# Three narrow attentions: products with values in pieces between transposition tiles, evacuated behind them

## What is computed

```python
attn = jnp.einsum('bkhd,bnhd->bhkn', q, kmat) / DH
attn = jnp.where(full_mask[:, None, None, :], attn, -jnp.inf)
attn = jax.nn.softmax(attn.astype(jnp.float32), axis=-1)
attn_out = jnp.einsum('bhkn,bnhd->bkhd', attn, v).reshape(b, k_len, H)
attn_out = attn_out @ out_w + out_b + residual
...
vh = jnp.concatenate([vh, jnp.broadcast_to(bias_v, (b, 1, H, K))], axis=1)   # layer 1
ctx = jnp.einsum('bhqt,bthk->bqhk', weights, vh).reshape(b, q_len, H * K)
return ctx @ wo + bo
```

## Time and profile before

| | us |
|---|---|
| median of three runs | 1074.5 |
| lowest and highest | 1072.48 and 1076.6 |
| the profiled execution | 1073.68 |
| its span, first to last instruction | 1071.9 |
| mean granted TensorE clock | 0.947 |

### The profile page before, as it was taken

How to read it: one execution, slowest core, us unless ns; L and a number is a source line. 1 busy time by engine, 2 the same in 40 slices (tenths; PEclk the granted TensorE clock), 3 DMA queues, 4 the chain that set the end, 5 groups by cost and what they waited for, 6 DMA issues and landing times. The chain is left out here.

```text
span 1071.9 us, 17946 instructions
## 1 busy us (share of the span) xinstructions
PE 946.0 (88%) x6616; PEld 802.6 (75%) x6616; DVE 774.2 (72%) x1625; ACT 604.4 (56%) x1371; POOL 312.3 (29%) x321
## 2 busy tenths in 40 slices
PE   4889886899999999999799999998487899779958
PEld 4766665788999999998689999997476666656647
DVE  3486766468878888886688888877674788558864
ACT  3587883236555655554455656555334787268842
POOL 3454550050221122221121122200004455445510
PEclk8899998999999999999899999999798799889989
DMA  4996005140110011111010011000306820394020
GB/s 147 273 232 97 2 1 197 60 159 1 40 40 5 36 41 40 41 40 41 1 40 6 35 40 40 1 1 1 124 1 158 208 46 2 106 242 64 1 85 20
DMA packets 39490, 72.71 MB, mean 68 GB/s; under 512 B 6534, under 2 KB 23944, under 8 KB 37228
## 3 DMA queue, kind: packets, MB, share of 16 engines
q1 hardware_dynamic: 39404, 71.56, 25.0%
HBM read 55.28 MB, written 16.27 MB: 67 GB/s over the span
## 5 line engine op out<-in xcount | busy, mean ns | idle before, releaser
L1316 ACT CAST L1a_probsT_hi<-L1a_bank 128x512 fp32r<-128x512 f32 x128 | 68.9, 589 | 84.6 <-PE L1a_bank L1194 84.5
L1152 POOL TENSOR_SCALAR L1a_wo_hi<-L1a_stage 128x512 fp32r<-128x512 f32 x16 | 10.4, 652 | 344.4 <-PE L1a_sums L74 336.5
L1351 ACT ACTIVATE L1a_probs<-L1a_scores,L1a_neg_max 128x512 f32<-128x512 f32 x128 | 86.8, 684 | 26.7 <-DVE L1a_bias_shifted L1441 22.1
L1437 DVE TENSOR_REDUCE L1a_top<-L1a_scores 128x2 f32<-128x1024 f32 x64 | 78.1, 1221 | 18.6 <-PE L1a_scores L74 18.6
L1374 DVE TENSOR_TENSOR L1a_probsT_lo<-L1a_bank,L1a_probsT_hi 128x512 fp32r<-128x512 f32 x128 | 82.0, 681 | 0.2
L1318 ACT ACTIVATE L1a_attended_hi<-L1a_bank,L1a_cols 128x256 fp32r<-128x256 f32 x64 | 30.5, 477 | 90.6 <-PE L1a_bank L74 90.6
L72 PE MATMUL L1a_bank<-L1a_probsT_hi,L1a_v_hi 128*128 128x256 f32 x256 | 73.1, 285 | 9.1 <-DVE L1a_probsT_lo L1374 9.1
L72 PE MATMUL L1a_bank<-L1a_w_hi,ctxT_hi 128*128 128x256 f32 x256 | 74.8, 292 | 0.3 <-DVE L1a_k_lo L1376 0.3
L417 POOL TENSOR_SCALAR L0a_probs<-L0a_probs,L0a_inverse 128x768 f32<-128x768 f32 x64 | 57.2, 906 | 57.8 <-DVE L0a_inverse L686 57.8
L74 PE MATMUL L1a_bank<-L1a_probsT_hi,L1a_v_lo 128*128 128x256 f32 x256 | 72.4, 283 | 0.0
L73 PE MATMUL L1a_bank<-L1a_probsT_lo,L1a_v_hi 128*128 128x256 f32 x256 | 72.4, 283 | 0.0
(11 more groups left out here) (410 smaller groups left out, 3083.4 us busy)
## 6 DMA issues: line engine op xcount, KB each, us to landing
L1a_stage<-in_L_w SPq DMA_DIRECT2D x15, 1024.0 KB, 4.8
L0m_fold_wq<-in_L_wqT SPq DMA_DIRECT2D x2, 2048.0 KB, 12.9
L0a_k_dram<-L0a_kT_hi SPq DMA_DIRECT2D x8, 384.0 KB, 10.2
L0a_k_stack<-L0a_k_dram SPq DMA_DIRECT2D x4, 576.0 KB
L0a_w_qkv<-L0a_k_dram SPq DMA_DIRECT2D x4, 576.0 KB
L0a_wide_wo<-in_L_wo SPq DMA_DIRECT2D x1, 2048.0 KB, 17.2
L0a_wide_wo<-in_L_wo SPq DMA_DIRECT2D x2, 1024.0 KB, 17.7
L0m_stage<-in_L_wm SPq DMA_DIRECT2D x4, 512.0 KB, 6.4
```

Of the source, the lines that this page charges most:

```text
L1316: nc.scalar.copy(out, source).then_inc(ring.hi_done, 1)
L1351: nc.scalar.activation(probs[:, g % 2, qt, :], scores[:, qt, :], ACT.Exp, bias=neg_max[:, g % 2, qt:qt + 1], accum_out=row_sum[:, g % 2, q ...
L1437: link(nc.vector.tensor_reduce(top[:, :], scores[:, :, :], AX.X, ALU.max))
```

## The change

A product is now split into `tj` pieces. For t = 5, 9, .. 29 (now `product_beside(t)`), PE writes transposition tile 0 of head t, piece 0 of the product, tile 1, piece 1, and so on. The product keeps one bank, but its job number comes behind the tiles of head t. On ACT and DVE its evacuation stands behind that of the tiles of head t. The values of the bias are split into one job for each of the two attentions of layer 1 (`bias_beside`, t = 14 and 15), in pieces as well, each with a copy of its own. `probsT` gets a sixth slot, since head t is written while the product still reads the unit.

```diff
-        TSLOTS = 5
+        TSLOTS = 6
...
-        def product_before(t):
+        def product_beside(t):
 
             return t // 4 - 1 if t % 4 == 1 and t >= 4 else None
 
 
-        BIAS_UNIT = 2
+        def bias_beside(t):
+
+            return t - 14 if cfg["bias_values"] and t in (14, 15) else None
+
         order = []
         for t in range(HEADS):
-            if product_before(t) is not None:
-                order.append(("V", product_before(t), 0))
-                if cfg["bias_values"] and product_before(t) == BIAS_UNIT:
-                    order.append(("B", 0, 0))
             order += [("T", t, c) for c in range(tj)]
+            if product_beside(t) is not None:
+                order.append(("V", product_beside(t), 0))
+            if bias_beside(t) is not None:
+                order.append(("B", bias_beside(t), 0))
         order.append(("V", units - 1, 0))
...
+            def values_of_bias(i, piece, pieces):
+                job = job_of["B", i, 0]
+                if piece == 0:
+                    pe.wait_ge(spread_ready, 1)
+                    pe.wait_ge(wide_loaded, 16 * 3)
+                    ring.wait_bank(pe, job)
+                for c in range(piece * 4 // pieces, (piece + 1) * 4 // pieces):
+                    for j in range(4):
...
                     last.then_inc(ring.full, 1)
+                    if unit is not None:
+                        product_v(unit, c, tj)
+                    if bias_layer is not None:
+                        values_of_bias(bias_layer, c, tj)
+
+            def product_v(unit, piece=0, pieces=1):
                 job = job_of["V", unit, 0]
-                ring.wait_bank(pe, job)
                 b, quad = divmod(unit, quads)
-                for back in range(ring.n):
-                    ring.wait_evacuated(pe, unit_copies(unit)[-1 - back])
-                for kt in range(nkt):
+                if piece == 0:
+                    ring.wait_bank(pe, job)
+                    for back in range(ring.n):
+                        ring.wait_evacuated(pe, unit_copies(unit)[-1 - back])
+                for kt in range(piece * nkt // pieces, (piece + 1) * nkt // pieces):
...
             def evacuate(t):
 
-                if product_before(t) is not None:
-                    high_v(product_before(t))
...
                 for c in range(tj):
                     if by_act(t, c):
                         job = job_of["T", t, c]
...
+                if product_beside(t) is not None:
+                    high_v(product_beside(t))
+                if bias_beside(t) is not None:
+                    job = job_of["B", bias_beside(t), 0]
+                    act.wait_ge(ring.full, job + 1)
+                    nc.scalar.copy(keep["bias_values"][:, bias_beside(t), :], ring.bank(job)[:, 0:D]).then_inc(ring.freed_by(job), 1)
...
                 if t >= 0:
-                    if product_before(t) is not None:
-                        low_v(product_before(t))
                     for c in range(tj):
                         if not by_act(t, c):
...
+                    if product_beside(t) is not None:
+                        low_v(product_beside(t))
```

More of the change, by code:

```diff
@@ L452, in _, with transpose_head @@
                 last.then_inc(ring.full, 1)
[L454 to L457, removed]
-                ring.wait_bank(pe, job)
[L459 to L467, removed]
+            def values_of_bias(i, piece, pieces):
[6 more added lines that the diff above has]
+                    for j in range(4):
+                        h = 4 * j + c
+                        last = nc.tensor.matmul(ring.bank(job)[32 * j:32 * j + 32, 0:D], spread[:, i, h, :],
+                                                wide_wo(i * H + h), start=c == 0, stop=c == 3)
+                if piece == pieces - 1:
+                    last.then_inc(ring.full, 1)
+            def transpose_head(g, unit, bias_layer):
                 pe.wait_ge(normed, 2 * g + 2)
@@ L476, in transpose_head @@
                     last.then_inc(ring.full, 1)
-            def product_v(unit):
+                    if unit is not None:
[3 more added lines that the diff above has]
+            def product_v(unit, piece=0, pieces=1):
                 job = job_of["V", unit, 0]
-                ring.wait_bank(pe, job)
                 b, quad = divmod(unit, quads)
-                for back in range(ring.n):
-                    ring.wait_evacuated(pe, unit_copies(unit)[-1 - back])
-                for kt in range(nkt):
+                if piece == 0:
[3 more added lines that the diff above has]
+                for kt in range(piece * nkt // pieces, (piece + 1) * nkt // pieces):
                     for j in range(4):
@@ L490, in product_v @@
                                                 moving, start=kt == 0, stop=kt == nkt - 1)
-                last.then_inc(ring.full, 1)
+                if piece == pieces - 1:
+                    last.then_inc(ring.full, 1)
             for g in range(HEADS + LAG):
@@ L508, in _ @@
                 if t >= 0:
-                    if product_before(t) is not None:
[L510 to L513, removed]
+                    transpose_head(t, product_beside(t), bias_beside(t))
             product_v(units - 1)
```

## The result

The changed kernel takes 1094.9 us (median of 4 runs, 1091.6 to 1098.4), the kernel before 1073.5 beside it (4 runs, 1067.4 to 1076.6): a ratio of 1.020, 95% interval 1.017 to 1.023. It is slower by 21.4 us. The forecast was 1099, its range 1083 to 1107.

The account below looks back on a forecast made before the run. It took PE to be near its limit in L0a, and ACT and DVE to bound L2a and L3a. Terms of 9.2 + 7.8 + 7.8 = 24.8 us on 1073.7 gave 1098.5, forecast as 1099, range 1083 to 1107.

Parts of the forecast that it names:

- first periods of L2a and L3a: First period of L2a and L3a, bank free: changes of form plus `low_v` make 0.8 us (0.5 to 1.1) each.
- Waiting for POOL, L0a: L0a: tile 0 now stands first and waits for POOL's multiplication, which the product used to cover; 0.36 us a period.
- Changes of form, L0a: L0a: three pairs of changes between transposition and product instead of one; two more at 0.27, 0.54 us a period.
- `low_v` ahead of the maxima, L0a: L0a: evacuation right before the next maxima starts them 1.10 us behind their scores, 0.45 us later each period.
- The seventh product and the end of L0a: L0a, t = 29: product ends later and DVE passes `low_v` before the last reciprocal; 1.5 us more.
- Bias values: L0a: bias values split over two heads lengthen the period by 3.05 us instead of 3.43, a gain of 0.4.
- The bank, L2a and L3a: L2a, L3a: piece 0 waits for a bank that ACT frees two exponentials later; maxima 1.06 us later, five periods 5.3.
- The ends of L2a and L3a: L2a, L3a, seventh product: late bank delays head 30's transposition, last product and output follow in series; 1.7 us each.
- The bank not late: Rival: ACT runs closer to PE, so L2a and L3a pay nothing and L0a pays 9.2; 1083 us, chance 0.11.
- Hidden: Rival: the waits fall into slack, above all in L0a, and earlier copies pay the rest; 1074 us, chance 0.05.
- faster: Rival: DVE's idle 1.21 us before `low_v` goes in 12 periods of L2a and L3a; 1060 us, chance 0.03.
- The clock falls: Rival: PE's clock drops at the new 1.2 to 1.4 us wait, 1.0 in 12 periods; 1111 us, chance 0.05.

## Why the prediction was right, and where it was off

The direction, the range and the main mechanisms were right. The sum was 24.8 us, and 21.4 were measured. A part of this closeness is luck: L0a came out 1.2 us above its sum, L2a and L3a together 3.1 below theirs. The step that is furthest off is the smallest in the argument: the first periods of L2a and L3a.

- **Waiting for POOL, L0a.** Predicted 0.36. Measured: from scores to tile 0 115.59 - 113.80 = 1.79, and before from scores to product 124.73 - 123.33 = 1.40; 0.39. Right.
- **Changes of form, L0a.** Predicted two pairs at 0.27, 0.54 in all. The two pairs cost 0.56 to 0.58 (pieces ahead of the tiles, whole products behind them), and three more pairs 0.86. But after has one entry more that shows: before, the one entry stood ahead of the product, in time in which tile 0 now waits for POOL anyway, so all three entries of after are visible. 4.76 - 4.01 = 0.75 is three entries and two exits. I had counted pairs, where I should have counted what stands behind the wait: 0.2 a period too little. The gaps that I expected in PE's rows are not there; they are in those of the weight loads.
- **`low_v` ahead of the maxima, L0a.** Predicted 0.45 (maxima 1.10 behind the scores). Measured: 1.05 behind them and 0.40 from scores to scores, and 0.38 come back when `low_v` is moved. Right, a little too high. The three together: 0.39 + 0.75 + 0.40 = 1.54, and 1.50 is the period's growth; predicted 1.35.
- **The seventh product and the end of L0a.** Predicted 1.5. From the last exponential to `w_out` 12.11 instead of 10.42: 1.7.
- **Bias values.** Their price fell from 3.43 to 3.16; predicted 3.05. Right in kind. The other form, whole and behind the tiles, shows what pieces took of it: 2.06 above its own period.
- **The bank, L2a and L3a.** Predicted +1.06 a period; measured +0.91, in both. The step that failed is the hand-over. I took the product's start, 0.21 behind ACT's copy, for the time from a copy to PE, and put it behind the new copy as well. But there PE was still at the scores issued at 865.88; the copy had been done. The rival of the bank that is not late was weighed with the same reading. A real hand-over is 0.05 (880.47 to 880.52). 1.06 - 0.16 = 0.90. The repaired bank gives 1.00 back.
- **The ends of L2a and L3a.** Predicted 1.7; from the last exponential to `w_out` 8.55 instead of 7.00: 1.55. The same 0.16 is in it.
- **The first periods of L2a and L3a.** Predicted +0.8 each. With five periods at 0.91 and the end taken out, 7.27 - 4.55 - 1.55 = 1.2 is left in L2a, and 5.23 - 6.10 = -0.9 in L3a. The waits of PE show what differs there, stretch of L2a to L3a, after:

```profile
PE L2a_scores L515 <- DMA L2a_q_stack<-L2a_q_dram: 7.2, 2, 3.9
PE L2a_bank L497 <- ACT L2a_probsT L585: 6.2, 6, 1.0
...
PE L3a_scores L515 <- DMA L3a_q_stack<-L3a_q_dram: 5.3, 2, 3.2
```

Before, the waits for these transfers were 5.1 and 6.8 us. The change moves no transfer. L2a's wait is 2.1 longer and L3a's 1.5 shorter, and in the experiments too these two stretches begin with waits of different length. So a part of L3a's 2.6 us and of the 1.4 elsewhere is this execution's share of luck with the transfers, not the change's. I can't say how it divides.

**The rivals.** *The bank not late* fell: PE waits 6.2 us for it in each of the two stretches, and repairing it gives 10 us back. *Hidden* and *faster* fell with it. What *faster* counted on, the idle 1.21 us of DVE before `low_v`, is still there (0.85). *The clock falls* did not happen in the profiled execution of the changed kernel, in these stretches behind the first product, but see the last section. The estimate that the prediction made from the Trainium skill's 175 ns (TensorE: Matmul & The Clock Gate, "Single matmul latency"), 0.35 for a pair and 1102 in all, is too high: six pieces gave 0.29 for each pair.

## What to carry to other kernels

In a ring of buffers the place in the order of jobs is also a choice of buffer: when a job moves behind two others, look up whose release it now needs, and when the engine that releases it comes to it. If that is late, the job can be given another place in the ring without moving any work, which gave 10 us here. Put long work of old data where the engine would wait for new data, not behind that wait, and don't let an evacuation stand directly in front of the operation that starts the next chain. Cutting work into pieces of another array form costs a fixed price for each change, which was hidden here only where the array had time to spare.

## What the runs showed of the hardware

- A change between full 128-column transposition tiles and 32-column quarter tiles costs about 0.15 us going in and 0.13 to 0.135 coming out, for pieces of 4 and of 8 matmuls alike (a matmul here is two of the records counted behind x). With all 24 matmuls in one, before, it was 0.12 coming out, and 0.16 going in from scores. PE's records show no idle time there; the price is in the steps between starts. The weight loads' records idle 0.17 us going in and 0.41 coming out. What the price consists of these runs don't separate.
- From the end of ACT's copy to the first matmul or weight load that waits for it 0.05 us pass (880.47 to 880.52; 888.26 to 888.31 with the other bank, where ACT's copy runs from 887.68 for 0.58).
- In the profiled executions of three of the eleven kernels of the study, five single periods in the middle of an attention are 1.0 to 1.6 us longer than their neighbours with no wait of their own. They hold a stretch at half clock. One of them, in L2a of the kernel with `low_v` one head later; columns as in the first fence, one us each row:

```profile
893.00:894.00 1.00, 0.81 (x5) 0.42 (x4) 1.00 (x3) 1.00 (x4) 0.50 (x2) 1.00 0.00 0
894.00:895.00 1.00, 0.01 (x3) 0.02 (x3) 1.00 (x3) 1.00 (x4) 1.00 (x2) 1.00 0.08 16
895.00:896.00 1.00, 1.00 (x12) 0.57 (x16) 0.50 (x2) 1.00 (x3) 0.50 (x2) 0.60 0.00 0
```

PE idles through 894.00 to 895.00 at its 1.03 us wait for the bank, and behind it the granted clock is 0.60 on the mean of one us and then 0.50, which is 1.2 GHz instead of 2.4; this period took 11.51 us, 1.58 more than its neighbours. Yet four kernels (the changed one, `low_v` one head later, six pieces, pieces ahead) have this wait six times in L2a and six times in L3a, 48 in all, and behind 45 of them the clock stays at 1.00. The other two of the five periods are in L0a, in the kernels with six pieces and with only the bank changed. There PE had waited 0.80 us for an exponential at 90 to 91 us, and the clock was at 0.50 from 94 us on; the wait for the bank is not in L0a at all. So the rival of the falling clock was not wrong in kind: the clock can fall behind waits of about 1 us, in some periods and some executions. What decides it in one period and not in the next these runs don't show.
